# First attention of a two-layer kernel: the low parts of the values get a matmul of their own

## The reference

```
q_r    = q_big @ W_qr                       # 16 heads, 256 query rows, 64 wide
k_r    = kv_r  @ W_kr                       # 1601 keys
scores = einsum('bhsr,bhlr->bhsl', q_r, k_r)
attn   = softmax(scores, axis=-1)
ctx_c  = einsum('bhsl,bld->bhsd', attn, kv_r)    # 64 wide
out    = (ctx_c through w_kc_kv, heads side by side) @ Wo.T
```

## Time and profile before

| | |
|---|---|
| time, median of 3 runs | 1670.37 us (1670.13 to 1671.88) |
| the profiled execution | 1672.2 us, its span 1670.3 us |
| mean granted TensorE clock | 0.977 |
| matmuls, and as many weight loads | 16127 |
| first attention, the steady loop | about 115 to 1170 us of the span |
| L819, L822 | 3328 matmuls each |

### The profile page before, as it was taken

One profiled execution on the slowest core, in us unless ns is written; L12 is line 12 of the kernel. 1 busy time (PEld: TensorE's weight loads), 2 busy tenths in 40 slices (PEclk: granted clock), 3 DMA queues, 4 the chain that ended last, 5 costly groups with the idle time before them and its releaser, 6 DMA issues. The chain is left out here.

```text
span 1670.3 us, 48690 instructions
## 1 busy us (share of the span) xinstructions
PE 1603.9 (96%) x16127; PEld 1300.0 (78%) x16127; DVE 1304.6 (78%) x3044; ACT 1015.0 (61%) x2024; POOL 1016.3 (61%) x970
## 2 busy tenths in 40 slices
PE   5889999999999999999999999999999899999998
PEld 4678888888888888888888888888787445555787
DVE  6888888888888888888888888888784668885223
ACT  5876767666667676666676767676322466664121
POOL 5338888888888888888878787878200224431321
PEclk8699999999999999999999999999999999999999
DMA  9721121121121122112112113412840011101344
GB/s 257 248 77 43 50 77 44 42 85 44 43 73 55 45 62 65 47 48 79 39 53 74 48 46 106 91 47 76 213 94 0 7 41 65 65 8 53 99 146 159
DMA packets 184808, 125.97 MB, mean 75 GB/s; under 512 B 107562, under 2 KB 171992, under 8 KB 184368
## 3 DMA queue, kind: packets, MB, share of 16 engines
q1 hardware_dynamic: 183216, 121.27, 26.4%
q0 software_dynamic: 1536, 3.99, 0.7%
HBM read 81.98 MB, written 24.48 MB: 64 GB/s over the span
## 5 line engine op out<-in xcount | busy, mean ns | idle before, releaser
L1177 POOL TENSOR_TENSOR c_rest<-c_prob 128x1024 f16<-128x1024 f32 (+1 forms) x513 | 796.7, 1574 | 223.2 <-ACT c_prob L965 213.1
L965 ACT ACTIVATE c_prob<-c_psS,ln,c_exp_scale 128x1024 f32<-128x1024 f32 (+1 forms) x514 | 536.8, 1044 | 236.6 <-PE c_psS L801 231.6
L1070 DVE TENSOR_REDUCE c_mxp<-c_psM 128x1 f32<-128x400 f32 (+1 forms) x1040 | 581.2, 572 | 108.0 <-PE c_psM L785 94.8
L801 PE MATMUL c_psS<-c_q,c_kk 128*128 128x256 f16 (+1 forms) x3350 | 512.6, 272 | 0.2 <-issue 0.2
L819 PE MATMUL c_psV<-c_vb,c_prob 128*128 128x129 f16 (+1 forms) x3328 | 404.0, 221 | 1.0 <-ACT c_acc L1019 1.0
L801 PEld LDWEIGHTS c_psS<-c_q,c_kk 128*128 128x128 f16 (+1 forms) x3350 | 321.7, 99 | 83.4 <-issue 0.4
L822 PE MATMUL c_psV<-c_vb,c_rest 128*128 128x65 f16 (+1 forms) x3328 | 380.8, 193 | 0.0
L785 PE MATMUL c_psM<-c_kkm,c_q 128*128 128x400 f16 (+1 forms) x1040 | 346.0, 333 | 4.1 <-DVE c_mxp L1070 3.0
L819 PEld LDWEIGHTS c_psV<-c_vb,c_prob 128*128 128x128 bf16 (+1 forms) x3328 | 308.0, 97 | 16.7 <-ACT c_acc L1019 1.3
L822 PEld LDWEIGHTS c_psV<-c_vb,c_rest 128*128 128x128 f16 (+1 forms) x3328 | 301.5, 99 | 22.1
L747 PE MATMUL c_psQ<-c_xb,c_w2s 128*128 128x256 f16 x1188 | 162.9, 274 | 5.3 <-PEq L163 4.2
(11 more groups left out here) (323 smaller groups left out, 2197.0 us busy)
## 6 DMA issues: line engine op xcount, KB each, us to landing
c_w2s<-w_scr SPq DMA_DIRECT2D x66, 256.0 KB, 2.6
c_ms<-m_scr SPq DMA_DIRECT2D x67, 192.0 KB, 2.4
c_w2s<-w_scr SPq DMA_DIRECT2D x66, 128.0 KB, 2.1
acc_scr<-c_acc SPq DMA_DIRECT2D x129, 64.0 KB
kv<-acc_scr SPq DMA_DIRECT2D x16, 512.0 KB, 6.5
m_w<-in_L_ffn_W SPq DMA_DIRECT2D x16, 352.0 KB, 3.7
c_vb<-V SPq DMA_DIRECT2D x27, 129.0 KB, 2.0
c_kk<-KK SPq DMA_DIRECT2D x27, 128.0 KB, 2.0
```

Source lines behind the costliest of these rows:

```text
L801: mm = pe.matmul(psS[g % 2][0:r, i * S:(i + 1) * S], src[:, (lo + i) * P:(lo + i) * P + r], mov[slot][:, :], start=(one == 0 and i % 2 == ...
L965: nc.scalar.activation(prob[g][0:r, 0:w], psS[g % 2][0:r, 0:w], ACT.Exp, bias=keep["ln1024"][0:r, :], scale=exp_scale[slot][0:r, :]).then_ ...
L1070: nc.vector.tensor_reduce(mxp[:, st, c:c + 1], psM[:, st, 0:CHUNKS[c][1]], AX.X, ALU.max).then_inc(mx_done, 1)
L1177: nc.gpsimd.tensor_tensor(rest[g][0:r, 0:w], prob[g][0:r, 0:w], high[0:r, 0:w], ALU.subtract).then_inc(rest_done, 1)
```

## The change

The PSUM columns of a half become `W` = 65 instead of 129: 64 columns for the sums and one for the sum of the row. The matmul of the high parts now streams the high values and the ones (65 columns), that of `rest` the same 65, and a third one, again with the high part of the probabilities as its stationary operand, streams the 64 low values onto the same first 64 columns. Each matmul comes with its weight load. The drain copies 130 columns, GpSimd's addition is gone and its function is renamed `sums`, and `summed` counts one a head.

```diff
-    W = 2 * DC + 1
+    W = DC + 1
...
-                sp.wait_ge(summed, 2 * n + 2)
-                sp.dma_start(t["acc_scr"][n], acc[(u + 1) % 2][:, :, DC:2 * DC]).then_inc(sent[(u + 1) % 2], 16)
+                sp.wait_ge(summed, n + 1)
+                sp.dma_start(t["acc_scr"][n], acc[(u + 1) % 2][:, :, 0:DC]).then_inc(sent[(u + 1) % 2], 16)
...
                     for st in range(ST):
                         c0 = (i - lo) * S + st * P
-                        pe.matmul(psV[:, st * W:(st + 1) * W], high[0:r, c0:c0 + P],
-                                  vb[0:r, i, :],
+                        out = psV[:, st * W:(st + 1) * W]
+                        pe.matmul(out, high[0:r, c0:c0 + P], vb[0:r, i, DC:DC + W],
                                   start=(i == 0 and st == 0), stop=False, skip_group_check=True)
-                        mm = pe.matmul(psV[:, st * W + DC:(st + 1) * W], rest[g][0:r, c0:c0 + P],
-                                       vb[0:r, i, DC:W],
+                        pe.matmul(out, rest[g][0:r, c0:c0 + P], vb[0:r, i, DC:DC + W],
+                                  start=False, stop=False, skip_group_check=True)
+                        mm = pe.matmul(out[:, 0:DC], high[0:r, c0:c0 + P], vb[0:r, i, 0:DC],
                                        start=False, stop=(i == LT - 1), skip_group_check=True)
...
-            def total(n, i):
+            def sums(n, i):
 
                 pool.wait_ge(pv_drained, n + 1)
-                nc.gpsimd.tensor_tensor(acc[i][:, :, DC:2 * DC], acc[i][:, :, DC:2 * DC], acc[i][:, :, 0:DC],
-                                        ALU.add).then_inc(summed, 1)
                 nc.gpsimd.tensor_copy(keep["rec"][:, bass.ds(n, 1), :].rearrange("p o s -> p (o s)"),
-                                      acc[i][:, :, 2 * DC]).then_inc(summed, 1)
+                                      acc[i][:, :, DC]).then_inc(summed, 1)
```

More of the change, by code:

```diff
@@ L725, in _ @@
             batch_steps(B - 1, 0)
-            sp.wait_ge(summed, 2 * N + 2)
-            sp.dma_start(t["acc_scr"][N], acc[1][:, :, DC:2 * DC]).then_inc(sent[1], 16)
+            sp.wait_ge(summed, N + 1)
+            sp.dma_start(t["acc_scr"][N], acc[1][:, :, 0:DC]).then_inc(sent[1], 16)
             for u in range(2):
@@ L1160, in _ @@
                     reduce_max(n + 2, 7)
-            dve.wait_ge(summed, 2 * H0 + 2)
+            dve.wait_ge(summed, H0 + 1)
             first = keep["rec"][:, 1:H0 + 1, :]
@@ L1202, in _ @@
                     rest_of(n, 3)
-                    total(n, (u + 1) % 2)
+                    sums(n, (u + 1) % 2)
                     rest_of(n + 1, 0)
-            total(N, 1)
+            sums(N, 1)
 class Norm:
```

## The result

| | before | after |
|---|---|---|
| median of plain runs, first chip | 1670.53 us (4 runs) | 1678.66 us (4 runs) |
| ratio, 95% interval | | 1.0048 [1.0033, 1.0063] |
| the same on another chip | 1664.88 us (11 runs) | 1670.84 us (6 runs), 1.0041 [1.0028, 1.0054] |
| span of the profiled execution | 1670.3 us | 1676.6 us |

The change makes the kernel slower, by 6 to 8 us. The forecast was 1674 in a range of 1664 to 1700, with 0.50 for slower.

The account below looks back on a forecast made before the run. It took TensorE's stream of columns as the bound. On the 1670.4 us median, GpSimd, ScalarE and SyncE added nothing; +2 ns a pair at 2.2 us per nanosecond gave +4 us: 1674, range 1664 to 1700.

Parts of the forecast that it names:

- TensorE's stream is the bound, and GpSimd's and ScalarE's relief is worth nothing: First attention's loop: TensorE's columns limit; GpSimd's 58.6 us and ScalarE's 14 us of saved work add nothing.
- The columns stay and a load and an issue are added; the loads don't bind: Value matmuls on TensorE: 194 columns before and after, three weight loads instead of two, 3328 more loads and issues.
- the stall: TensorE waits about 145 ns before group 1's values in every second head, behind ScalarE's and GpSimd's fixed 5.2 us latency.
- The rival of the load as bound: Weight loads pace the value matmuls: 44 ns a load gives 1807 us, 35 gives 1718; chance 0.14.
- What a trio costs: The three value matmuls per key tile and query half: 90.2 ns against 88 for the former pair, +2.
- one loss: Likeliest case: one 3 ns loss per trio of value matmuls, 90.2 ns, +4 us, 1674; chance 0.33.
- two losses: Rival: 3 ns lost at both high-part matmuls of a trio, +5 ns a pair, 10.9 us, 1681; chance 0.20.
- How a nanosecond reaches the end: 34 of two heads' 52 pairs count, in 64 double heads: 2.2 us for each nanosecond per pair.
- Relief of the stall by GpSimd: Rival: less GpSimd work removes the 145 ns wait in 64 heads, 9.3 us; with faster trios 1658; chance 0.08.
- A pause behind a run of values, for want of instructions: Sign before maxima or scores that TensorE's queue ran short, 6 instructions in 90 ns instead of 4 in 88.

Follow-up runs that it names:

- e5_no_sum: Kernel before with only GpSimd's addition of the two PSUM parts left out: ratio 1.0010 [0.9999, 1.0022].
- e2: Changed kernel, first and third matmul of each trio loading the contiguous remainder instead of the strided high part: 1669.90 us against 1664.54 for the kernel before.
- e8: Changed kernel with the two matmuls of the same high part next to each other, remainder last: 1672.36 us against 1664.88 for the kernel before.
- e7: e6 with the column of ones streamed for the first tile only, other matmuls exactly 64 columns: 88.7 ns a trio, two heads 16.600 us.
- e6: Changed kernel with value rows laid 384 bytes apart, on multiples of 128 bytes: 1672.84 us against 1667.56 for the kernel before, 90.8 ns a trio.
- e9: Kernel before with each score matmul of 256 columns made as two of 128: 1666.38 us against 1664.88.
- b_scores_first: Kernel before with the next head's first two score matmuls moved ahead of the values of group 1: 1660.96 us against 1667.56, ratio 0.9961.

## Why the prediction was right, and where its number was off

- *TensorE's stream is the bound, and GpSimd's and ScalarE's relief is worth nothing*: right. e5_no_sum takes GpSimd's part alone and changes nothing; the idle time before its subtractions grew instead, from 1.06 to 1.47 us there. ScalarE's part had no run of its own: TensorE waited for the drain once in the loop, 1.0 us before and 0.8 after, so there was nothing to gain. SyncE waited 86.7 instead of 114.1 us for the store's semaphore in the same stretch, and 236.2 instead of 201.8 for TensorE's progress behind it (L627), as the forecast had it.
- *The columns stay and a load and an issue are added; the loads don't bind*: right. But for the first after the stall, no gap in the long runs lay more than some 9 ns over streaming, and neither a contiguous (e2) nor a repeated load (e8) made a trio faster. The rival of the load as bound, 44 or 35 ns each, is out: a matmul with its load takes 30.6 ns in runs of 36. One sign of that rival did appear, starts 0.04 us apart in the long runs. They aren't the loads: e7 has the same loads as e6 and nearly no such start. The Trainium skill, "TensorE: Matmul & The Clock Gate", gives 107 ns for such a load in its section "LDWEIGHTS (loading the stationary operand)" and about half of that in the one on weight-path modes. The traces don't agree with either figure, at 30.6 ns for a load with its matmul, and the measurement decides.
- *What a trio costs*: the term that was mis-sized. I took one loss of 3 ns and a fixed cost of 2.1 ns a matmul: 90.2 ns against 88, 2 ns more. Measured 91.7 against 88.4, 3.3 ns, between the cases "one loss" and "two losses". Its parts: 194 columns are 80.8 ns either way. The fixed cost is 2.5 ns where e9 measured it; if it is the same at 65 columns, which no run shows by itself, 5 of a pair's 7.6 ns beyond the columns and 7.5 of a trio's 10.9 are that. The irregular loss is the remainder: 2.6 ns for the pair, 3.4 for the trio. So 2.5 of the 3.3 ns are the plain price of one matmul more, and 0.8 an irregular loss that grew. The forecast had 0.4 ns too little for the first and nothing for the second. It lay in its range and on the right side; the half of it that was missing was not foreseen.
- *How a nanosecond reaches the end*: right. 34 x 3.3 x 64 = 7.2 us; two heads are 0.111 us longer, x 64 = 7.1; the spans differ by 6.3 and the medians by 8.1 and 6.0. The stall swallowed its share, 65 ns, where 18 x 3.3 = 59 were due and 36 were forecast.
- *Relief of the stall by GpSimd*: out (e5). That TensorE's work put into the gap can take it, b_scores_first shows: 6.6 us.
- *A pause behind a run of values, for want of instructions*: not seen; TensorE goes on with the maxima at 611.66, 0.03 us after the last value matmul.

## What to carry to other kernels

Where one engine streams without a gap, count its instructions as well as its columns: cutting a matmul in two at the same columns cost 2.5 ns even with the load hidden, and 3.3 where the pieces were 65 and 64 wide, thousands of times. Work taken off an engine that idles in front of its critical chain buys nothing, however much it is; look for the fixed latency that the bound engine waits on, and put other work of the bound engine into that wait. And compare on one chip: the kernel before alone differed by up to 6 us between four of them, as much as the effect, while the distance of starts agreed to 0.1 ns.

## What the hardware showed unexpectedly

- Score matmuls of 128 and 256 columns, in dense runs with a new load each, cost columns/2.4 + 2.5 ns in the mean (55.9 and 109.2). Value matmuls of 64 to 66 columns cost 2.9 to 3.9 ns beyond their columns: 61.5 ns for a pair of 65, 91.7 for the trio, 88.7 when nearly all are 64 wide. A value matmul of 129 columns in the kernel before took 59.0 ns, 5.2 beyond its columns, and the one of 65 behind it 29.4.
- With 65 or 66 columns the excess isn't spread: most starts stand at 28 to 31 ns and one in three to five at 32 to 36. With rows of exactly 64 columns on 128-byte multiples (e7) the late ones are 3%.
- Which one is late depends on the place in the run, not on the operand: the start behind the second value matmul of a run is 33 to 35 ns away in the median whether that matmul reads the remainder, the high part or the other half, and 29 only in e7. With rows on 128-byte multiples and 65 columns the pattern repeats every six matmuls. What sets it stays open: strided loads, repeated columns and row addresses alone are excluded as the main cause, the width of the row takes part.
- A granted clock of 1.00, the 2.4 GHz level, held through the loop in all kernels, also with 36 narrow matmuls in a row.
